# A state space layer without the product with the zero state, its entry weights loaded one stage earlier, and attention's stack copies all started by SyncE

## The chip, the cores and the metric

One Trainium2 chip, one core. The kernel is one launch for the whole model; the metric is the device time of that launch in microseconds (us), the median of the runs shown. Engines: TensorE (PE: matmuls; PEld: its weight loads), VectorE (DVE), ScalarE (ACT), GpSimd (POOL) and SyncE (SP, which only starts transfers here). The profile is one execution taken by the hardware profiler.

## The reference

Two rows of 1024 tokens with 512 channels go through four layers, each as `x = x + layernorm(layer(layernorm(x)))`: causal attention (32 heads of 16), a gated FFN whose weights are multiplied by low rank factors (FFN0), a state space layer, and a gated FFN (FFN1). The state space layer is what the change is mostly about:

```
proj = hidden @ in_proj_w.T            # gate | x,B,C | dt
hbc  = silu(conv4(x,B,C))              # causal, 4 taps per channel
dt   = softplus(dt + dt_bias); dA = exp(-dt * exp(A_log))
state = state * dA + (dt * x) B        # state0 = 0, for each token
y    = C . state + D * x
out  = (rmsnorm(y) * norm_weight * silu(gate)) @ out_proj_w.T
```

It has 64 heads of 64 in 8 groups, each group with one B and one C of 128.

## The kernel before, in words

Everything is fp32; a product is made of three fp32r matmuls from values split into hi and lo (hi x hi, lo x hi, hi x lo), so 12 matmuls of 512 columns make one product with K = 512. Each engine has its own program; semaphores order them. The outer loop runs over the 2 rows of the batch, and in each over the stages ATT, PROJ, FFN0, STEPS_DT, MAMBA, FFN1. `leave(engine, b, phase)` counts an engine out of a stage; `enter(engine, b, phase)` waits until all five engines have left the stage before. It is needed where a buffer of a new stage lies over one of an old stage.

**State space, MAMBA.** `m_group(g, first, last)` of each engine does one group of 8 heads in 8 chunks c of 128 tokens (TT = 8). A chunk on PE is, in this order (L986 to L1046): decays (L976, L977), B turned and the C-B product into bank 3 (L998, L999), the convolved projections of this or the next group (`PROJ_AT`: two in chunks 0 and 2 of each half, one in 1 and 3; `wide`, L928), with the last normed chunk turned in between (`turn_out`, L940), the product of C with the state (L1020, bank 6), the gate (`wide`, L928) with the 8 heads (L959, bank 7) between its matmuls, the out projection of the chunk before (`project_out`, L928, bank 3) with the next x turned in between (`turn_x`, L949), and the state update (L1046, bank 6). A bank of the two that projections and gate share is free when the use two before it has been read (`bank_read`): ahead of the gate of chunk 0 that is the convolution (DVE, L1684 to L1687) of the chunk's first projection.

What the other engines do for a chunk: ACT copies x_tm (L1283) and b_tm (L1286), takes the exponent of the decays (L1262), the first tap of a convolution (L1247), yt_hi (`turned_hi`, L1257), the silu's tanh (L1252), scales the state product into yv in 8 pieces (L1315), the gate's tanh (L1318), and the sum of squares (L1321); then splits weights (`split_hi`, L1236; wy is first scaled, L1234). In chunk 0 the first two splits of wy wait until the out projection is done. DVE: `masked` (L1703, L1706), convolutions, yt_lo (`turned_lo`, L1711), yv plus bank 7 (L1764), plus xd (L1767), gate (L1769), `gather` of the out projection from bank 3 into Y (L1717, L1719), state plus bank 6 (L1788), yn (L1791). In chunk 0 of a group DVE clears the state (L1739). POOL: xdt, xw, xd (L2061 to L2067), lo parts of weights (L2038), state times decay (L2078), decay terms (L2044), and the root of the mean square (L2090, L2092).

**The entry, STEPS_DT.** PE takes the product of the first half of the tokens with the dt weights (`steps_in(0)`), then six projections `project(0, 0, ft)`, with `steps_turn(0)` ahead of ft = 1, the turning of the second half's normed tokens, `steps_in(1)` behind ft = 2, `steps_turn(1)` behind ft = 3 and the decay sums (L902) behind ft = 4. SP loads wdt, dt_bias, a_log, d_skip (L552), cpar (L562) and m_raw (L560) after all engines have left FFN0. POOL then splits wdt (L1889, L1891).

**Attention.** Heads go by quads t = 0 to 7, two quads for each f = 0 to 3. Queries and keys of f are projected in four blocks (f, 0..3) of 12 matmuls (L595 to L597); weights come by `load_qk(f)` (L461, L463) and are split by POOL, the query half before (f, 0), the key half before (f, 2). `stack(t)` copies their hi and lo parts, SBUF to SBUF, into rows of stack_q and stack_k by 24 transfers (L309). The stacks of t = 2, 3 use the second buffers, which lie over the value weights, so they wait for `v_used`. SP starts all copies but those of t = 3, which ACT starts between its own steps. The maxima of a quad are built from 48 `piece` products (L803) each reduced by DVE (L1602, L1607), turned (L810) and brought into the stack by `put_maxima` (L479), on which the first score (L826) of the quad waits. `attention_order()` writes the order of all blocks out by hand; 48 pieces of quad 0 and 6 of quad 1 come before the first score. part_hi of f = 1 lies over probs, so ACT's first exponents (L1213) wait for the stacks of t = 2 and 3.

## Time and profile before

| | before |
|---|---|
| median of 3 runs | 4067.1 us (4065.34 to 4072.07) |
| profiled execution, time | 4082.54 us |
| its span | 4080.8 us |
| granted clock of TensorE, mean | 0.925 |
| PE busy | 3809.3 us, 93% |
| DVE busy | 2732.6 us, 67% |
| ACT busy | 1686.5 us, 41% |
| POOL busy | 1805.8 us, 44% |
| chain that ended last | PE 81%, issue 7%, DVE 4% |

A share of busy time is an average over stages with different limits. A row of a timeline gives start, duration, engine, line, operation, what it writes <- what it reads, and in brackets the idle time of the engine before it with what ended it. Durations of matmuls include their pipeline, so neighbours overlap: their distance is the start of the next less the start of this one. Two lines name one thing where a helper is shared: L595 to L597 are all products of attention and FFN, L928 all wide products of the state space layer.

### The profile page before, as it was taken

The page shows a single profiled execution, that of the slowest core. Times are in us where ns is not written, and L with a number is a line of the kernel's source. Part 1 is how long each engine was busy: PE and PEld are TensorE (multiplying, and loading weights), DVE is VectorE, ACT ScalarE, POOL GpSimd, SP SyncE. Part 2 cuts the span into 40 slices and gives each one's busy share as a digit, 9 for nine tenths or more (in the row PEclk, how much of TensorE's full clock was granted, in tenths as well). Part 3 has the DMA queues.
Part 4 walks back from the last instruction along what each step waited for, and adds up shares of the span by engine and source line. Part 5 has one row for each costly group of instructions (what it writes and reads, how often), then busy time and mean ns, then how long its engine had stood idle before and what let it go on. Part 6 is the DMA issues. An engine that isn't in the chain of part 4 may idle for free.

```text
span 4080.8 us, 61636 instructions
## 1 busy us (share of the span) xinstructions
PE 3809.3 (93%) x18088; PEld 2768.1 (68%) x18088; DVE 2732.6 (67%) x5102; ACT 1686.5 (41%) x3555; POOL 1805.8 (44%) x1993
## 2 busy tenths in 40 slices
PE   7899899799999999979979998996999999999797
PEld 5444588577777777767754446874777777777586
DVE  4576455678777787764546754556778777787545
ACT  1344411355555555541214443114555555555412
POOL 2111444266555665643221124433666655665432
PEclk9767799899999999989987768998999999999899
DMA  4120111011010111001051301101111100110111
GB/s 104 31 49 27 34 48 40 24 37 35 29 27 25 31 36 28 23 26 57 24 116 27 61 15 33 48 32 34 27 37 31 31 21 25 36 34 18 52 39 36
DMA packets 84630, 151.95 MB, mean 37 GB/s; under 512 B 16488, under 2 KB 18616, under 8 KB 84432
## 3 DMA queue, kind: packets, MB, share of 16 engines
q1 hardware_dynamic: 80784, 142.23, 13.1%
q10 hardware_dynamic: 3648, 7.34, 0.7%
q8 instruction: 92, 1.51, 0.1%
q14 instruction: 106, 0.87, 0.1%
HBM read 119.37 MB, written 4.19 MB: 30 GB/s over the span
## 4 chain that ended last, share of the span: by engine, by line
PE 81%; issue 7%; DVE 4%; POOL 2%; DVEq 2%; ACT 1%; POOLq 1%; DMA 1%; SPq 1%; ACTq 0%; PEldq 0%; PEld 0%
PE banks L928 30%; PE banks L595 8%; PE banks L596 7%; PE banks L597 7%; PE banks L845 5%; PE banks L959 4%; PE banks L826 4%; PE banks L803 3%; PE banks L1020 2%; PE banks L1046 2%; PE banks L976 1%; PE banks L977 1%; PE banks L949 1%; PE banks L940 1%; DVEq L1690 1%
## 5 line engine op out<-in xcount | busy, mean ns | idle before, releaser
L1687 DVE SCALAR_TENSOR_TENSOR conv<-banks,cpar,conv 128x509 f32<-128x509 f32 (+2 forms) x576 | 428.1, 743 | 123.0 <-ACT conv L1247 106.0
L959 PEld LDWEIGHTS banks<-xdt,decay 128*128 128x128 f32 x2048 | 393.9, 193 | 65.8 <-DVE decay L1706 11.2
L1213 ACT ACTIVATE probs<-banks 128x1024 f32<-128x1024 f32 (+3 forms) x384 | 296.7, 809 | 328.9 <-PE banks L826 328.3
L1474 DVE TENSOR_TENSOR Y<-banks,Y 128x512 f32<-128x512 f32 x368 | 253.1, 691 | 164.3 <-PE banks L597 163.0
L595 PE MATMUL banks<-xhi,f_hi 128*128 128x512 f32 x800 | 325.8, 407 | 30.9 <-POOL f_lo L1891 16.6
L959 PE MATMUL banks<-xdt,decay 128*128 128x64 f32 x2048 | 342.0, 249 | 12.7 <-DVE decay L1706 9.3
L2012 POOL TENSOR_SCALAR_AFFINE_SELECT probs<-probs 128x256 f32<-128x256 f32 x256 | 103.8, 406 | 536.6 <-ACT probs L1213 536.2
L803 PE MATMUL banks<-stack_k,stack_q 48*128 48x512 f32 (+3 forms) x768 | 320.5, 500 | 13.8 <-DVE mx L1607 6.8
L1602 DVE CUSTOM_DVE_ANT_0 banks<-banks,mask_qk 128x128 f32<-128x128 f32 (+3 forms) x512 | 249.3, 500 | 117.7 <-PE banks L803 113.2
L596 PE MATMUL banks<-xhi,f_lo 128*128 128x512 f32 x800 | 320.8, 401 | 0.0
L597 PE MATMUL banks<-xlo,f_hi 128*128 128x512 f32 x800 | 320.6, 401 | 0.0
L928 PE MATMUL banks<-xhi,wx_hi 128*128 128x512 f32 x720 | 310.4, 431 | 0.0
L826 PE MATMUL banks<-stack_q,stack_k 50*128 50x512 f32 (+3 forms) x768 | 292.0, 487 | 5.7 <-DVE mx L1602 3.0
L928 PE MATMUL banks<-xhi,wx_lo 128*128 128x512 f32 x720 | 295.9, 411 | 0.0
L928 PE MATMUL banks<-xlo,wx_hi 128*128 128x512 f32 x720 | 295.5, 410 | 0.0
L826 PEld LDWEIGHTS banks<-stack_q,stack_k 50*128 50x128 f32 x768 | 169.0, 249 | 168.3 <-issue 125.8
L928 PE MATMUL banks<-wg_hi,xhi 128*128 128x512 f32 x512 | 262.0, 512 | 21.8 <-DVE conv L1687 21.8
L2090 POOL TENSOR_SCALAR rg<-ss 128x1 f32<-128x1 f32 x128 | 25.1, 196 | 541.3 <-ACT banks L1321 541.3
L1889 POOL TENSOR_SCALAR f_hi<-f_raw 128x512 fp32r<-128x512 f32 x150 | 96.5, 643 | 324.2 <-PE banks L597 301.9
L928 PE MATMUL banks<-wg_lo,xhi 128*128 128x512 f32 x512 | 238.3, 465 | 0.0
L1132 ACT CAST h_hi<-hf 128x512 fp32r<-128x512 f32 x100 | 62.2, 622 | 408.2 <-DVE hf L1459 408.2
L928 PE MATMUL banks<-wy_hi,yt_hi 128*128 128x512 f32 x512 | 229.4, 448 | 0.7 <-POOL wy_lo L2038 0.7
(229 smaller groups left out, 10402.1 us busy)
## 6 DMA issues: line engine op xcount, KB each, us to landing
m_raw<-in_w_mamba SPq DMA_DIRECT2D x224, 256.0 KB, 2.6
f_raw<-in_w_ffn SPq DMA_DIRECT2D x50, 768.0 KB, 4.6
x_next<-in_x SPq DMA_DIRECT2D x6, 1024.0 KB, 8.8
wqk_raw<-in_w_attn SPq DMA_DIRECT2D x8, 512.0 KB, 3.7
stack_q<-part_hi SPq DMA_DIRECT2D x64, 64.0 KB, 2.4
stack_k<-part_hi SPq DMA_DIRECT2D x64, 64.0 KB, 2.5
X<-in_x SPq DMA_DIRECT2D x4, 1024.0 KB, 6.5
out_y<-X ACTq DMA_DIRECT2D x4, 1024.0 KB, 5.1
```

Source lines behind the costliest of these rows:

```text
L595: pe.matmul(dst, a_hi(kt), w_hi(kt), start=first, stop=False)
L596: pe.matmul(dst, a_lo(kt), w_hi(kt), start=False, stop=False)
L597: return pe.matmul(dst, a_hi(kt), w_lo(kt), start=False, stop=last)
L803: pe.matmul(bank[RING_BANK[use]][:, 0:cols], stack_q[buf][base:base + ROWS, h, i * P:(i + 1) * P], stack_k[buf][base:base + ROWS, h, s * H ...
L826: r = pe.matmul(bank[h][:, at:at + w], stack_k[buf][base:base + ROWS + 2, h, j * P:(j + 1) * P], stack_q[buf][base:base + ROWS + 2, h, s * ...
L845: r = pe.matmul(bank[6][32 * h:32 * h + VW, lo:HALF], V[:, j, QUAD * t + h, :], probs[n % 2][:, h, at:at + w], start=j == 0, stop=j == CPH ...
L928: r = pe.matmul(dst, a(kt), w(kt), start=n == 0, stop=n == 3 * KT - 1)
L959: r = pe.matmul(bank[7][:, h * MP:(h + 1) * MP], decay[:, h, :], xdt[:, h * MP:(h + 1) * MP], start=True, stop=True, skip_group_check=True)
L1213: act.activation(probs[n % 2][:, 2 * p:2 * p + 2, 0:w], banks[:, 2 * p:2 * p + 2, 0:w], ACT.Exp, scale=1.0 / HD ** 0.5).then_inc(exp_done[ ...
L1474: dve.tensor_tensor(Y[:, i, :], bank[6 + i % 2], Y[:, i, :], ALU.add).then_inc(f["dn_used"], 1)
L1602: dve.tensor_tensor_reduce(out=src, in0=src, in1=mask_qk[:, HALF - cols:HALF], scale=1.0, scalar=NEG, op0=ALU.add, op1=ALU.max, accum_out= ...
L1687: r = dve.scalar_tensor_tensor(out=rest, in0=src[:, 0:HALF - lag], scalar=cpar[:, o:o + 1], in1=rest, op0=ALU.mult, op1=ALU.add)
```

## The change

- The state of a group starts at zero, so chunk 0 leaves out the clearing, the product of C with the state, its scaling on ACT, one of DVE's two adds and the decay of the state on POOL; the state after chunk 0 is a copy of bank 6. The semaphores' counts follow (7 a group where there were 8).
- In chunk 0 of every group but a row's first, PE does the out projection of the chunk before ahead of the gate. ACT's `turned_hi` and DVE's `turned_lo` therefore come ahead of the first convolution.
- wdt, its three rows, cpar and the first two m_raw are loaded by SP at the end of FFN0 and wdt is split by POOL in FFN0; the buffers have places outside FFN0's. In STEPS_DT, PE turns the second half's tokens after ft = 1 and turns its steps after ft = 2, and ACT and DVE follow.
- In attention a block has 4 pieces (12 blocks), "values" 5 to 7 alternate with (1, 2), (1, 3), and the 6 pieces of quad 1 stand between (2, 3) and (3, 0). POOL splits query and key weights of an f in one operation each, after the last block of the f before. SP starts the copies of t = 3, and `load_qk(3)` goes ahead of `stack(2)`.

The diff, cut to what the text speaks of, with the common indentation taken off (the rest names the buffers' new places and the same counts):

```diff
-    for at, (first, second) in enumerate(blocks_left):
+    blocks_left = [("values", 3), (1, 0), ("values", 4), (1, 1), ("values", 5), (1, 2), ("values", 6), (1, 3),
+                   ("values", 7), (2, 0), (2, 1), (2, 2), (2, 3), None, (3, 0), (3, 1), (3, 2), (3, 3)]
+    for block_ in blocks_left:
+        if block_ is None:
+            yield "maxima", 0
+            yield from some(2)
+            yield "maxima_out", 0
+            yield from some(AHEAD - 2)
+            continue
+        first, second = block_
         values = first == "values"
...
-        if (first, second) == (2, 3):
-            yield "maxima", 0
-        if (first, second) == (3, 0):
-            yield "maxima_out", 0
-        if 9 <= at < 14:
-            yield "copies", 5 * (at - 9), min(5 * (at - 8), 24)
-        count = 3 if at < 9 else 7 if at < 12 else 2 if (first, second) in ((3, 0), (3, 3)) else 0
-        if (first, second) == (3, 3):
-            yield from some(AHEAD - 2)
-        else:
-            yield from some(min(count, 2))
+        count = min(PER_BLOCK, len(pieces) - (NQ - 1) * NP) if len(pieces) > (NQ - 1) * NP else 0
+        yield from some(min(count, 2))
         yield ("values_out", second) if values else ("proj_lo", first, second)
-        yield from some(count - 2 if count > 2 else 0)
+        yield from some(count - min(count, 2))
...
-            for n in range(QUAD * 6):
-                copy_part(sp, t, n)
+            for h in range(QUAD):
+                src = slice(HD * (QUAD * par + h), HD * (QUAD * par + h + 1))
+                for dst, which, parts in ((stack_q[f % 2], 0, (part_hi, part_hi, part_lo)),
+                                          (stack_k[f % 2], 1, (part_hi, part_lo, part_hi))):
+                    for r, part in enumerate(parts):
+                        at = 64 * par + HD * r
+                        sp.dma_start(dst[at:at + HD, h, :].bitcast(F32),
+                                     part[f][src, which, :].bitcast(F32)).then_inc(stacked[f % 2][par][h], 16)
...
+        load_qk(3)
         held(sp, v_used, b + 1)
         ones_in(1)
         stack(2)
-        load_qk(3)
+        stack(3)
         put_maxima(0)
...
         for at in STACK_AT:
             sp.dma_start(lrc_raw[at:at + RANK, :], lr0_const).then_inc(F[0]["lr_const"], 16)
         ffn_loads(0, w_ffn0, NF0, True)
-        leave(sp, b, FFN0)
-        enter(sp, b, STEPS_DT)
-
+        enter(sp, b, FFN0)
         for dst, src in ((wdt_raw[:], w_dt), (dtb[:], dt_bias), (alog[:], a_log), (dsk[:], d_skip)):
             sp.dma_start(dst, src).then_inc(dt_w_in, 16)
-        leave(sp, b, STEPS_DT)
-
+        sp.dma_start(cpar[:], conv_par[0]).then_inc(cpar_in, 16)
...
-        sp.dma_start(cpar[:], conv_par[0]).then_inc(cpar_in, 16)
-        for n in range(CT):
-            m_load(0, n, n, n < 2)
+        for n in range(2):
+            m_load(0, n, n, True)
+        leave(sp, b, FFN0)
+        enter(sp, b, STEPS_DT)
+        for n in range(2, CT):
+            m_load(0, n, n)
+        leave(sp, b, STEPS_DT)
...
-                    pe.wait_ge(wqk_ready, b * 8 + 2 * f + which + 1)
+                if use_f == 0 and part == 0:
+                    pe.wait_ge(wqk_ready, b * 8 + 2 * f + 2)
...
-                pe.wait_ge(state_ready, it + 1)
-                if c == 0:
-                    pe.wait_ge(inter_used, START + it)
-                pe.matmul(bank[6][:], xbc[s][:, XT + 1, ck], state[:], start=True, stop=True
-                          ).then_inc(inter_done, 1)
+                if c:
+                    pe.wait_ge(state_ready, sm + c)
+                    pe.matmul(bank[6][:], xbc[s][:, XT + 1, ck], state[:], start=True, stop=True
+                              ).then_inc(inter_done, 1)
+
+                def out_ahead():
+                    if c == 1:
+                        pe.wait_ge(m_split, b * (MG * W_PER_G) + g * W_PER_G + W_PER_G)
+                    pe.wait_ge(bc_ready, START + it + 1)
+                    ahead = (c + 1) % CPH != 0
+                    project_out(it - 1, {2 + 2 * k: lambda k=k: turn_x(it + 1, c + 1, k) for k in range(XT)}
+                                if ahead else {})
+
+                if c == 0 and not start:
+                    out_ahead()
...
                 at += 1
 
-                if not start:
-                    if c == 1:
-                        pe.wait_ge(m_split, b * (MG * W_PER_G) + g * W_PER_G + W_PER_G)
-                    pe.wait_ge(bc_ready, START + it + 1)
-                    ahead = (c + 1) % CPH != 0
-                    project_out(it - 1, {2 + 2 * k: lambda k=k: turn_x(it + 1, c + 1, k) for k in range(XT)}
-                                if ahead else {})
+                if c:
+                    out_ahead()
 
                 if c < TT - 1:
-                    pe.wait_ge(inter_used, START + it + 1)
+                    pe.wait_ge(inter_used, START + sm + c)
...
-            if ft == 2:
+            if ft == 1:
                 norm_turn(b * 4 + 2, 2, half(1))
                 normed(b * 4 + 2, 1)
                 steps_in(1)
-            if ft == 3:
+            if ft == 2:
                 steps_turn(1)
             if ft == 4:
                 decay_sums()
...
         for what, *arg in ORDER:
-            if what == "copies":
-                first, last = arg
-                if first == 0:
-                    held(act, v_used, b + 1)
-                    held(act, part_lo_ready, b * 16 + 8)
-                    act.drain()
-                for n in range(first, last):
-                    copy_part(act, 3, n)
-            elif what == "proj_hi":
...
                 turned_yet = start
+                if c == 0 and not start:
+                    turned_hi(it - 1)
                 while uses[at][0] == "proj":
...
@@ -1294,7 +1294,8 @@
                     s1 = 1 if n < CT else 0
                     before_conv(bank[at % 2], p0 + n, n, s1)
                     if not turned_yet:
-                        turned_hi(it - 1)
+                        if c:
+                            turned_hi(it - 1)
                         turned_yet = True
...
                 act.wait_ge(yn_ready, START + it)
-                act.wait_ge(inter_done, START + it + 1)
-                act.wait_ge(gt_ready, (b * MG + g) * 2 + c // CPH + 1)
-                for h in range(HPG):
-                    own = slice(h * MP, (h + 1) * MP)
-                    r = act.activation(yv[:, own], bank[6][:, own], ACT.Identity, scale=gt[:, EC, c, h:h + 1])
-                r.then_inc(inter_used, 1)
+                if c:
+                    act.wait_ge(inter_done, START + (b * MG + g) * (TT - 1) + c)
+                    act.wait_ge(gt_ready, (b * MG + g) * 2 + c // CPH + 1)
+                    for h in range(HPG):
+                        own = slice(h * MP, (h + 1) * MP)
+                        r = act.activation(yv[:, own], bank[6][:, own], ACT.Identity, scale=gt[:, EC, c, h:h + 1])
+                    r.then_inc(inter_used, 1)
...
+        act.wait_ge(dt_w_in, (b + 1) * 64)
+        act.activation(neg_a[:], alog[:], ACT.Exp)
         held(act, cpar_in, (b * MG + 1) * 16)
         for n in range(2):
             split_hi(wx_hi[:, n, :], n, 0)
-        act.wait_ge(dt_w_in, (b + 1) * 64)
-        act.activation(neg_a[:], alog[:], ACT.Exp)
         normed_y(b * 4 + 1, half(1))
         for n in range(2, 4):
             split_hi(wx_hi[:, n, :], n, 0)
         first_conv(0)
+        normed_x(b * 4 + 2, 2, half(1))
         first_conv(1)
         first_tanh(0)
-        normed_x(b * 4 + 2, 2, half(1))
...
-            held(dve, inter_done, START + (b * MG + g) * TT)
-            dve.memset(state[:], 0.0).then_inc(state_ready, 1)
...
                 turned = start
+                if c == 0 and not start:
+                    turned_lo(it - 1)
+                    turned = True
...
-                dve.wait_ge(inter_used, START + it + 1)
-                dve.wait_ge(intra_done, START + it + 1)
-                dve.tensor_tensor(yv[:], yv[:], bank[7], ALU.add)
-                dve.drain()
-                dve.wait_ge(pool_x, START + it + 1)
-                dve.tensor_tensor(yv[:], yv[:], xd[:], ALU.add).then_inc(y_ready, 1)
+                if c == 0:
+                    dve.wait_ge(intra_done, START + it + 1)
+                    dve.wait_ge(pool_x, START + it + 1)
+                    dve.tensor_tensor(yv[:], xd[:], bank[7], ALU.add).then_inc(y_ready, 1)
+                else:
+                    dve.wait_ge(inter_used, START + sm + c)
+                    dve.wait_ge(intra_done, START + it + 1)
+                    dve.tensor_tensor(yv[:], yv[:], bank[7], ALU.add)
+                    dve.drain()
+                    dve.wait_ge(pool_x, START + it + 1)
+                    dve.tensor_tensor(yv[:], yv[:], xd[:], ALU.add).then_inc(y_ready, 1)
...
+                if c == 0:
+                    dve.wait_ge(st_mm, START + sm + 1)
+                    dve.tensor_copy(state[:], bank[6]).then_inc(state_ready, 1)
+                elif c < TT - 1:
                     dve.wait_ge(st_mm, START + sm + (c + 1))
-                    dve.wait_ge(state_dec, sm + (c + 1))
+                    dve.wait_ge(state_dec, (b * MG + g) * (TT - 2) + c)
                     dve.tensor_tensor(state[:], state[:], bank[6], ALU.add).then_inc(state_ready, 1)
...
+        steps_copy(0)
         add_y(b * 4 + 1, half(1))
         moments_x(b * 4 + 1, 1)
-        steps_copy(0)
         first_conv(0)
+        norm_lo(b * 4 + 2, half(1))
         first_conv(1)
         first_silu(0)
-        norm_lo(b * 4 + 2, half(1))
         steps_copy(1)
...
+        if i == 0:
+            held(pool, dt_w_in, (b + 1) * 64)
+            split(wdt_hi[:], wdt_lo[:], wdt_raw[:]).then_inc(dt_w_ready, 1)
...
         for what, *arg in ORDER:
-            if what == "proj" and arg[1:] in ([0, 0], [2, 0]):
-                f, which = arg[0], arg[1] // 2
+            if what == "proj" and arg[1:] == [0, 0]:
+                f = arg[0]
                 held(pool, wqk_in, (b * (NQ // 2) + f + 1) * 32)
                 if f > 0:
-                    held(pool, ring_done, b * RING + RING_ENDS.index(("proj", f - 1, 2 * which + 1)) + 1)
-                split(wqk_hi[:, which, :], wqk_lo[:, which, :], wqk_raw[:, which, :]).then_inc(wqk_ready, 1)
+                    held(pool, ring_done, b * RING + RING_ENDS.index(("proj", f - 1, 3)) + 1)
+                split(wqk_hi[:], wqk_lo[:], wqk_raw[:]).then_inc(wqk_ready, 2)
...
-                    pool.wait_ge(state_ready, it + 1)
-                    pool.wait_ge(inter_done, START + it + 1)
-                    pool.tensor_tensor(by_head(state[:]), by_head(state[:]), per_head(gt[:, ED, c, :]),
-                                       ALU.mult).then_inc(state_dec, 1)
+                    if c:
+                        pool.wait_ge(state_ready, sm + c)
+                        pool.wait_ge(inter_done, START + sm + c)
+                        pool.tensor_tensor(by_head(state[:]), by_head(state[:]), per_head(gt[:, ED, c, :]),
```

## Rows read from the trace of the kernel before

**Rows 1.** The page: busy time by engine; PE's granted clock by slice, in tenths.

```profile
PE 3809.3 (93%) x18088; PEld 2768.1 (68%) x18088; DVE 2732.6 (67%) x5102; ACT 1686.5 (41%) x3555; POOL 1805.8 (44%) x1993
...
PEclk9767799899999999989987768998999999999899
```

**Rows 2.** Waits of PE: waiting line <- releaser: total us, count, mean us.

```profile
PE banks L928 <- DVE conv L1687: 21.8, 14, 1.6
```

**Rows 3.** Windows, one group: us; PE, PEld, DVE, ACT, POOL; PEclk, DMA, GB/s.

```profile
945.00:1070.00 125.00, 123.42 (x616) 96.06 (x615) 98.43 (x152) 66.95 (x169) 75.92 (x77) 1.00 0.11 30
```

**Rows 4.** Timeline of PE, chunks 0 and 1 of one group.

```profile
952.70 1.02 PE L1020 MATMUL banks<-state,xbc 128*128 128x512 f32 x2
...
955.30 0.49 PE L928 MATMUL banks<-wg_hi,xhi 128*128 128x512 f32 x1 [1.58 <-DVE conv L1687]
...
959.90 0.48 PE L928 MATMUL banks<-wy_hi,yt_hi 128*128 128x512 f32 x1
...
963.21 1.02 PE L1046 MATMUL banks<-xw,b_tm 128*128 128x512 f32 x2
...
965.00 0.27 PE L998 MATMUL banks<-ident,xbc 128*128 128x128 f32 x1
...
967.44 0.27 PE L940 MATMUL banks<-ident,yn 128*128 128x128 f32 x1
...
974.01 0.47 PE L928 MATMUL banks<-wy_hi,yt_hi 128*128 128x512 f32 x1
```

**Rows 5.** Timeline of DVE, the same chunks.

```profile
955.03 0.68 DVE L1711 TENSOR_TENSOR yt_lo<-banks,yt_hi 128x512 fp32r<-128x512 f32 x1
...
960.20 0.69 DVE L1764 TENSOR_TENSOR yv<-yv,banks 128x512 f32<-128x512 f32 x1 [0.45 <-PE banks L959]
...
963.41 0.69 DVE L1719 TENSOR_TENSOR Y<-banks,Y 128x512 f32<-128x512 f32 x1 [1.16 <-PE banks L928]
...
973.19 0.68 DVE L1711 TENSOR_TENSOR yt_lo<-banks,yt_hi 128x512 fp32r<-128x512 f32 x1
```

**Rows 6.** Timeline of ACT, the same chunks.

```profile
963.51 0.72 ACT L1234 ACTIVATE m_raw<-m_raw,cpar 128x512 f32<-128x512 f32 x1 [1.10 <-PE banks L928]
...
966.13 0.58 ACT L1283 COPY x_tm<-banks 128x512 f32<-128x512 f32 x1
```

**Rows 7.** Timeline of PE, entry to the state space layer.

```profile
761.74 0.66 PE L595 MATMUL banks<-xhi,wdt_hi 128*64 128x512 f32 x1 [4.82 <-POOLq L277]
...
766.89 0.63 PE L595 MATMUL banks<-xhi,wx_hi 128*128 128x512 f32 x1
...
786.22 0.44 PE L595 MATMUL banks<-xhi,wdt_hi 128*64 128x512 f32 x1 [1.40 <-DVE xlo L1434]
```

**Rows 8.** Timeline of DVE, the same entry.

```profile
766.31 2.81 DVE L1441 TENSOR_TENSOR X<-X,Y 128x512 f32<-128x512 f32 x4 [4.05 <-ACT Y L1098]
...
792.38 0.69 DVE L1814 TENSOR_TENSOR dt_in<-banks,dtb 128x512 f32<-128x512 f32 x1 [2.50 <-PE banks L896]
```

**Rows 9.** Timeline of ACT, the same entry.

```profile
779.57 1.51 ACT L1112 ACTIVATE xn<-X,shift,rstd 128x512 f32<-128x512 f32 x2
```

**Rows 10.** Timeline of SP's queue, attention.

```profile
61.40 1.15 SPq L309 DMA_DIRECT2D stack_q<-part_hi  x2
...
76.77 0.59 SPq L309 DMA_DIRECT2D stack_k<-part_hi  x1
...
82.77 2.43 SPq L485 DMA_DIRECT2D stack_k<-ones  x4
...
102.57 0.38 SPq L461 DMA_DIRECT2D wqk_raw<-in_w_attn  x1
```

**Rows 11.** Timeline of PE, attention.

```profile
110.40 0.79 PE L595 MATMUL banks<-xhi,wqk_hi 128*128 128x512 f32 x1 [7.33 <-POOL wqk_lo L1891]
...
127.57 0.49 PE L826 MATMUL banks<-stack_q,stack_k 50*128 50x512 f32 x1 [1.52 <-DVE mx L1602]
```

**Rows 12.** Tile wqk_raw: durations in ns (min/median/max), first to last start in us.

```profile
L1891 POOL TENSOR_TENSOR wqk_lo<-wqk_raw,wqk_hi x16: 1260/1281/1298, 20.9 to 2138.3; 128x512 fp32r<-128x512 f32 x16
```

More of the change, by code:

```diff
@@ L158, in build @@
         with ExitStack() as s:
+            wdt_raw = sb("wdt_raw", [P, KT, MH], stack=s)
+            wdt_hi = sb("wdt_hi", [P, KT, MH], F32R, stack=s)
+            wdt_lo = sb("wdt_lo", [P, KT, MH], F32R, stack=s)
+            dtb = sb("dtb", [P, MH], stack=s)
+            alog = sb("alog", [P, MH], stack=s)
+            neg_a = sb("neg_a", [P, MH], stack=s)
+            dsk = sb("dsk", [P, MH], stack=s)
+        with ExitStack() as s:
             EC, WE, ED, DTH, AHI, ALO = range(6)
@@ L162, in build @@
             with ExitStack() as s2:
+                cpar = sb("cpar", [P, CT * (MK + 1) + XT], stack=s2)
                 m_raw = sb("m_raw", [P, 2, D], stack=s2)
@@ L169, in build @@
                 wy_lo = sb("wy_lo", [P, XT, D], F32R, stack=s2)
-                cpar = sb("cpar", [P, CT * (MK + 1) + XT], stack=s2)
                 gt = sb("gt", [P, 6, TT, HPG], stack=s2)
@@ L2030, in _ @@
                 enter(pool, b, STEPS_DT)
-                held(pool, dt_w_in, (b + 1) * 64)
-                split(wdt_hi[:], wdt_lo[:], wdt_raw[:]).then_inc(dt_w_ready, 1)
                 leave(pool, b, STEPS_DT)
```

24 lines of the change are left out of this document (5 added, 19 removed).

## The prediction

> **What bounds the kernel now.** I began with the page: TensorE (PE) is busy 93% of the span and its chain is 81% PE, so time can go only where PE waits, where it does needless work, or where its clock is low. The clock row says where the last is: from slice 2 to slice 5 (102 to 510 us, the attention of the first batch) 7, 6, 7, 7 tenths, and 9 in nearly all the state space layer [rows 1]. Then the waits of PE; the one that comes back evenly is 14 times 1.56 us, 21.8 in all, on VectorE's (DVE) convolution at L928 [rows 2]. One group takes 125 us, of which PE is busy 123.4 at full clock, so that wait is all its idle [rows 3]: there the layer is bound by PE. The timelines of the three places that the diff touches follow; the second batch repeats the first in all of them.
>
> State space, chunk 0 of a group [rows 4 to 6]: the product with the zero state starts at 952.70, then PE idles 1.58 until conv has emptied the gate's bank; gate 955.30 to 959.90 (4.60 us), out projection to 963.21 (3.31 us). Entry to the state space layer: PE waits 4.82 us for weights which SyncE (SP) loads only after FFN0, then runs at half clock (12 matmuls from 761.74 to 766.89, 0.43 us apart; at full clock they are 0.23 apart, as 963.21 minus 959.90 over 12, less four small turns, shows too) [rows 7]. Attention: PE waits 7.33 us at 110.40 because the last query and key weights were loaded at 102.57, behind 24 stack copies; the first score is at 127.57 [rows 10, 11].
>
> **Part 1, group heads (14 of the 16 groups).** From 952.70 to the state update at 963.21 PE now takes 10.51 us. Afterwards: out projection 3.31 from 952.70 to 956.0, gate 4.60 to 960.6. What must be ready: yt_lo, which now precedes the convolution (turned_hi 0.58 on ScalarE (ACT), 0.68 on DVE, so about 951.4); the gate's bank, whose convolution moves 0.6 later for the same reason, its end from 955.0 (where yt_lo starts, [rows 5]) to 955.65, still under the projection. So 2.6 us go: 1.58 wait and some 0.95 product (from the 10.51, less wait, gate and projection, 1.0). The memset, eight ACT scalings, one DVE add and POOL's decay multiply go too; each lay beside PE and I give them nothing by themselves.
>
> What is late next, in chunk 1. (a) PE needs bank 3 at 965.00, 1.8 after the state update begins, so at 962.4 after; DVE empties it 4.2 after the gate's end now (963.41 + 0.69), but 1.2 of that was waiting for the projection and 0.7 the second add, so 962.8 or 962.9 after: a new wait of 0.45. (b) ACT splits wy from 963.51 and then copies x_tm at 966.13; its start goes only to 962.3 (gate's end, tanh and add, square 0.8), 1.2 earlier where PE is 2.6 earlier. x_tm is done at 965.5; PE wants it at 965.35 or, with (a), later: 0.2. (c) The same ACT chain starts the decay exponent, DVE's masked product and convolution, and yt_lo, which ended at 973.87 just before PE's projection at 974.01. It ends at 972.3 after, PE is there at 972.1: 0.3. Together 0.95 of 2.6 comes back; 1.65 x 14 = **23.1 us**. Ends: 1.0 (all of the idle returns, only the product goes) and 2.6 (nothing returns); I take the value that the chain gives, near the middle.
>
> **Part 2, the two first groups.** There PE waits in the gate for DVE's masked product, which is not moved: the dropped product hides behind that wait, worth 0. One DVE add less (0.69 [rows 5]) lies in the chain to x_tm, on which PE then waits: 0.7 x 2 = **1.4**, ends 0 and 1.9.
>
> **Part 3, entry.** Loads of wdt, the three rows, cpar and the first two m_raw go into FFN0, behind the last FFN load on SP; nothing of FFN0 is queued behind them. POOL's split of wdt follows the last FFN split, where POOL has nothing due until the next variance: 0, at most its 1.2 us. DVE's step copy now precedes the add, so the turn no longer waits for the add and its statistics. PE's first step product starts at about 758.4 instead of 761.74. What ends next is the layer norm of the second half. DVE's add begins at 766.31 [rows 8]; the root that it hangs on comes 1.9 earlier, since on POOL the split of wx ahead of it is over sooner and the variance, ready at 762, ends the wait. So the statistics end at 770.4, the root at 771.8, and the turned tiles, which took 6.65 from the first xn at 779.57 [rows 9] to 786.22, take about 6.2 without a convolution and silu between them: second step product at 778.0 instead of 786.22. It comes after a wait of 5 us, so I take half clock for it (5.1, as in rows 7), then projection 2 (2.8), the turn (0.5): dt_in at 786.0 instead of 792.38 [rows 8]. Everything after it (softplus, decay sums, convolutions 3 to 5) hangs on dt_in, so 6.4 x 2 = **12.8**. Ends: 4.8 (only the wait for weights) and 8.5 (full clock).
>
> **Part 4, attention.** load_qk(3) goes ahead of stack(2), so the wait of 7.33 shrinks: both halves of f=2 are split after (1,3), under values 7; f=3 is split after (2,3), 3.7 us on POOL (two halves of 0.62 + 1.28 [rows 12]) beside maxima and six pieces (2.5): about 1.2 of wait, projections from 106 to 117.5. But the first score also needs put_maxima(0), and the first exponent needs stack(3), whose buffer source is probs. SP issues these in order. 24 copies take 61.40 to 77.36, 0.66 each [rows 10]. v_used falls at 82.77 now; with "values 7" one block later and four pieces a block it is 88.8. Ones 2.5, stack(2) and stack(3) 48 x 0.65 = 31.2, maxima 1.2, landing 2.1: first score at **125.8** instead of 127.57. So 1.8 x 2 = 3.6 gained; PE idles 8 us before it. The second batch starts up to 1.9 later as the query half no longer goes first (0 to 1.9; 0.8 taken). Full clock in the first 1.7 us of scores may be lost: 0.5 each. Sum **1.8**, ends a loss of 8 (copies 0.75 each, SP's queue as the bound) and a gain of 19 (rival 2).
>
> Here a rule speaks against a row. The Trainium skill, "DMA: Bandwidth & Descriptors", section "Issuing engines are not separate DMA queues", says that starting transfers on several engines saves only sequencer time, usually small beside the DMA. By it moving ACT's 24 copies to SP costs about nothing, which is rival 2; rows 10 give 0.66 of queue time each, and 24 in a row are not small. Another, "TensorE: Matmul & The Clock Gate", section "HAM oscillation", has PE come back slow after a wait; the scores run at a low clock already [rows 1], so by it the sum would lose no more than the 0.5 a batch taken above.
>
> **Sum.** 23.1 + 1.4 + 12.8 + 1.8 = 39.1 us. The profiled execution took 4082.5 with a span of 4080.8, so 4043.4; the median of the three runs shown is 4067.1, 15.4 below it, and its forecast is **4028**.
>
> **Rivals.** (1) Chunk 1 has more slack than I read: all 2.6 stays, 14 x 0.95 = 13.3 more, 4015. For it: DVE works beside a less busy POOL; against: rows 5 and 6 leave it under 0.2. (2) SP's queue does not end last; first score after the projections, at 118: 7.8 x 2 more, 4012. Against: rows 10. (3) The waits of chunk 1 eat all the idle: 14 x 0.95 for the product, so 9.8 less gain, 4038. For it: three chains (a to c) are each tight, and POOL's au_lo too. (4) Slower: attention loses clock. Its granted clock of 0.67 over slices 2 to 4 [rows 1] means a third of 306 us at 2.4 GHz, the rest at 1.2. The idle before the scores and a new order of pieces could move which stretches are granted. If a third of those 102 us per batch went to the low level, PE's work in them would take 34 us more, 68 in all, less 39: 4096. It decides from 20 us a batch. Against: both batches show nearly the same pattern though they start differently.
>
> **How the numbers follow.** Forecast 0.55, rival 1 0.14, rival 2 0.06, rival 3 0.19, rival 4 0.06 (slower by over 0.2% in 0.04 of it). A measurement tells about 0.2%, 8.1 us, from no change. Every case but rival 4 gains over 8.1 us; I keep 0.01 of them for the band, where their errors could add up. Faster 0.93, same 0.03, slower 0.04. The forecast's own spread is 12 us either way (part 1 from 1.2 to 2.4 a group, part 3, some us of attention's clock); with rivals 1 and 3 taken in and the outer part of 2 and 4 left out the range is 4008 to 4046.
>
> **What would show it.** No L1020 in chunk 0 and no idle ahead of the gate; instead short waits at L998 on the gather of Y, at L940 on x_tm and ahead of L928 on yt_lo in chunk 1; groups every 123.3 us (125.0 would refute part 1). The first wdt product close behind the last xlo, a_all some 6 us sooner. In attention two full trains of 24 copies on SP, and PE idle some 8 us before the first score, released by mt_lo; if it is released by DVE or starts at 118, part 4 is wrong. I am wrong altogether if attention's PEclk tenths fall, or if chunk 1 idles over 2 us.

## The result and the profile after

| | before | after |
|---|---|---|
| median | 4069.59 us (4 runs, 4065.34 to 4074.09) | **4004.05 us** (4 runs, 4000.12 to 4016.49) |
| ratio | | 0.9844, 95% interval 0.9819 to 0.9869 |
| profiled execution: span, mean granted clock | 4080.8, 0.925 | 4000.4, 0.939 |

65.5 us less; the forecast was 39.1 less, 4028, with a range of 4008 to 4046. The result lies 4 us below that range. Measured again beside the experiments, the changed kernel took 4018.8, 4014.0 and 4021.1 (medians on three chips): all 19 of its executions have a median of 4016.5 and a mean of 4014.0, and 68 of the kernel before 4070.1 and 4070.2. So the first four lie some 12 us below the rest of the evidence, and the gain to be explained is 56 us in the mean. The page of after, parts 1 and 2 (before: [rows 1]):

```profile
PE 3750.0 (94%) x18056; PEld 2736.6 (68%) x18056; DVE 2683.5 (67%) x5070; ACT 1664.6 (42%) x3427; POOL 1788.6 (45%) x1961
...
PEclk9867999899999999999997779998999999999899
```

PE is busy 59 us less, though only 32 matmuls fewer run. The clock row says most of why: slices 2 to 5 stood at 7, 6, 7, 7 and stand at 8, 6, 7, 9 here. The timelines of PE, cut at the same instructions in both profiled executions, give the time by stage (both batches), and windows of 4 us the time at 1.2 GHz within it:

| stage | before, us | after, us | at 1.2 GHz, before | after |
|---|---|---|---|---|
| attention's first product to its second score | 97.4, 98.8 | 95.9, 95.8 | 10, 15 | 6, 11 |
| to the last score | 311.3, 308.1 | 288.6, 302.6 | 198, 188 | 135, 172 |
| to the end of FFN0 | 313.7, 313.6 | 312.2, 312.0 | 24, 24 | 14, 14 |
| to the first step product | 9.2, 9.2 | 5.8, 5.8 | 4, 4 | 1, 1 |
| to the first state update | 74.7, 74.7 | 71.1, 71.1 | 30, 30 | 30, 30 |
| to the last state update | 961.9, 961.9 | 946.3, 948.0 | 3, 3 | 0, 3 |
| to the end of FFN1 | 241.8, 241.8 | 240.3, 242.0 | 27, 27 | 24, 27 |

28 of the 80 us between these two executions lie in the score stretch (the row "to the last score"), in which the diff moves nothing: there PE was 79 us less at 1.2 GHz.

**A group.** One group in the windows (before: [rows 3]), then PE's timeline from its last chunk (before: [rows 4]):

```profile
926.85:1049.85 123.00, 122.47 (x614) 95.62 (x614) 95.05 (x150) 65.72 (x160) 74.98 (x75) 1.00 0.11 31
```

```profile
1026.18 1.02 PE L1020 MATMUL banks<-state,xbc 128*128 128x512 f32 x2
...
1049.85 0.65 PE L1052 MATMUL banks<-xw,b_tm 128*128 128x512 f32 x1
...
1051.99 0.33 PE L999 MATMUL banks<-ident,xbc 128*128 128x128 f32 x1
...
1054.64 0.33 PE L940 MATMUL banks<-ident,yn 128*128 128x128 f32 x1
...
1061.57 0.50 PE L928 MATMUL banks<-wy_hi,yt_hi 128*128 128x512 f32 x1 [0.20 <-POOL wy_lo L2050]
```

Groups take 122.9 where they took 124.8. No L1020 stands in chunk 0 and nothing waits ahead of the gate. From the state update, B is turned 2.14 later (1.79 before), the normed chunk 4.79 (4.23), the projection 11.72 (10.80): the waits that the forecast named (a), (b) and (c) cost 0.35, 0.21 and 0.36, together 0.92, of which 0.95 was forecast. Only (c) ends with another engine than forecast: POOL's lo part of wy, and DVE's yt_lo had ended only 0.08 before it.

**The entry and the scores.** PE's step products, DVE's dt_in, then the two places of attention (before: [rows 7, 8, 11]):

```profile
732.72 0.69 PE L595 MATMUL banks<-xhi,wdt_hi 128*64 128x512 f32 x1 [1.40 <-DVE xlo L1436]
...
752.57 0.69 PE L595 MATMUL banks<-xhi,wdt_hi 128*64 128x512 f32 x1 [1.40 <-DVE xlo L1436]
```

```profile
760.05 0.69 DVE L1825 TENSOR_TENSOR dt_in<-banks,dtb 128x512 f32<-128x512 f32 x1 [2.46 <-PE banks L896]
```

```profile
106.04 0.28 PE L810 MATMUL banks<-ident,mx 128*32 128x128 f32 x1 [3.90 <-DVE mx L1614]
...
125.53 0.78 PE L826 MATMUL banks<-stack_q,stack_k 50*128 50x512 f32 x1 [5.18 <-DMA stack_q<-mt_lo]
```

```profile
122.61 0.52 SPq L477 DMA_DIRECT2D stack_q<-mt_hi  x1
123.17 0.59 SPq L477 DMA_DIRECT2D stack_q<-mt_lo  x1
```

FFN0 ends 25.60 earlier after (last product 726.94, not 752.54). On the clock of before the three entry rows stand at 758.32, 778.17 and 785.65, where 758.4, 778.0 and 786.0 were forecast. The first score was forecast at 125.8 and starts at 125.53, behind SP's 48 copies. PE idles 5.18 us ahead of it where some 8 were forecast, as 3.90 already went at the turn of the maxima.

In the trace of before, though, a score had already started at 124.82. The one at 127.57 that I took for the first [rows 11] is the second, with four of the six pieces of quad 1 and a wait between the two:

```profile
124.82 0.50 PE L826 MATMUL banks<-stack_q,stack_k 50*128 50x512 f32 x1
```

So the first score of the first batch came later with the change, not earlier. Second against second score, from the batch's first product, the gain is 1.5 and 3.0 us in the two batches.

### The profile page after: what moved, and what is told of

It reads as the page before. It is cut to its first block, busy times and chain, and to the rows that moved or that the text cites. A ratio compares the mean times of both kernels' runs of the same rounds, so it can differ in the third digit from the quotient of the medians.

```text
span 4000.4 us, 61382 instructions
## 1 busy us (share of the span) xinstructions
PE 3750.0 (94%) x18056; PEld 2736.6 (68%) x18056; DVE 2683.5 (67%) x5070; ACT 1664.6 (42%) x3427; POOL 1788.6 (45%) x1961
## 3 DMA queue, kind: packets, MB, share of 16 engines
q1 hardware_dynamic: 82320, 145.38, 13.6%
## 4 chain that ended last, share of the span: by engine, by line
PE 77%; issue 8%; POOL 5%; DVE 3%; SPq 2%; POOLq 1%; ACT 1%; DMA 1%; DVEq 1%; ACTq 0%
PE banks L928 29%; PE banks L595 8%; PE banks L596 7%; PE banks L597 7%; PE banks L845 4%; PE banks L959 4%; PE banks L826 4%; PE banks L803 3%; PE banks L1052 2%; PE banks L1020 2%; POOL wy_lo L2050 2%; SPq L470 1%; PE banks L949 1%; PE banks L976 1%; PE banks L977 1%
## 5 line engine op out<-in xcount | busy, mean ns | idle before, releaser
L826 PE MATMUL banks<-stack_q,stack_k 50*128 50x512 f32 (+3 forms) x768 | 279.5, 469 | 15.0 <-DMA stack_q<-mt_lo 12.7
```

Source lines behind the costliest of these rows:

```text
L826: r = pe.matmul(bank[h][:, at:at + w], stack_k[buf][base:base + ROWS + 2, h, j * P:(j + 1) * P], stack_q[buf][base:base + ROWS + 2, h, s * ...
```

## The experiments

All kernels' executions, 183 in all, lie on parallel lines of time against mean granted clock: 0.001 of clock is 2.5 us (least squares with one slope; scatter about the lines 2.4 us). "Equal clock" below is a kernel's distance to the kernel before, read between two such lines at one clock, so that what the mean clock did is taken out. Its uncertainty (one standard error) is 0.6 us for the changed kernel and 0.7 to 1.1 for the others.

| kernel | runs | mean us | mean clock | equal clock |
|---|---|---|---|---|
| before | 68 | 4070.2 | 0.9295 | 0 |
| changed (first runs, e4, e9, e15) | 19 | 4014.0 | 0.9329 | -47.4 |
| e1 attention alone | 12 | 4058.0 | 0.9320 | -5.8 |
| e2 heads alone | 6 | 4043.8 | 0.9298 | -25.5 |
| e3 entry alone | 8 | 4049.6 | 0.9311 | -16.5 |
| e12 heads and entry | 5 | 4025.3 | 0.9298 | -44.1 |
| e11 buffers moved | 10 | 4063.9 | 0.9304 | -4.0 |
| e7 product dropped | 6 | 4091.2 | 0.9233 | +5.5 |
| e8 projection ahead | 12 | 4067.9 | 0.9304 | +0.1 |
| e5, e16 copies by ACT | 9 | 4006.7 | 0.9340 | -52.1 |
| e6 maxima later | 6 | 4018.4 | 0.9312 | -47.5 |
| e10 query half first | 5 | 4009.5 | 0.9316 | -55.3 |
| e13 pieces late | 5 | 4020.8 | 0.9306 | -46.5 |
| e14 pieces early | 12 | 4055.6 | 0.9337 | -4.0 |

### One part at a time: e1, e2, e3, e4

The kernel before with the diff's attention parts alone (e1), its `m_group` parts alone (e2), its buffers and STEPS_DT parts alone (e3), and the whole again (e4).

> The kernel before with the attention part of the change alone. Theory A: the gain beyond the forecast is made by the attention part, whose new order gives the score stretch more of the full clock; then this kernel gains 15 to 22 us and PEclk of the scores is 0.72 to 0.77 where before it was 0.68 and 0.70. Theory B: the clock of the score stretch varies from execution to execution or with its start, whatever the order; then only the earlier scores count (1.3 us a batch), it gains 1 to 5 us, and the granted clocks of its runs lie among those of the kernel before.

Ratio 0.9978 (0.9960 to 0.9996), 4056.5 median: 12.2 us less in the mean, of which 5.8 at equal clock and the rest by a clock higher by 0.0025, so between A and B.

> The kernel before with the state space groups' part alone (no product with the zero state, out projection ahead of the gate). Both theories: groups every 122.9 us instead of 124.8, 14 x 1.92 = 27 us, and 1 to 4 for the two first groups, so 27 to 31 us. If it gains 35 or more, the clock of a stretch that it does not touch went with it (theory B). The forecast on record had 24.5.

0.9935 (0.9912 to 0.9959). Groups take 123.1, 25.5 us at equal clock. Both theories asked for 27 or more; the forecast's 24.5 was nearer.

> The kernel before with the entry part alone (weights and rows loaded in FFN0, steps turned earlier). Both theories: 3.4 us before the first step product and 3.6 behind it, per batch, so 13 to 15 us; the forecast on record had 12.8. Theory B allows 5 us more or less by the clock of attention.

0.9947 (0.9928 to 0.9966). 16.5 us at equal clock. By the stages 12.6 of them lie between the end of FFN0 and the first state update (3.4 and 3.4 in the first batch, 3.5 and 2.4 in the second); and the groups, not touched, took 124.63 instead of 124.81.

> The changed kernel once more, as the sum to which e1 to e3 are compared on one chip. Theory A: e1 + e2 + e3 add up to it within 5 us (near 65 us), and its scores have PEclk over 0.72 in both batches. Theory B: its total varies by 10 us with the clock, and the parts sum to 45 to 50 only.

0.9867 (0.9842 to 0.9892), 4018.8. At equal clock the parts sum to 47.8 and the whole is 47.4: they add up, and to less than the first result said. Windows over the scores of the first batch, of the first profile of the changed kernel and of e4, the same program:

```profile
125.50:414.70 289.20, 275.65 (x1529) 124.32 (x1529) 196.86 (x615) 147.58 (x190) 57.09 (x127) 0.77 0.18 36
```

```profile
125.50:432.40 306.90, 296.25 (x1530) 131.50 (x1528) 197.97 (x615) 147.73 (x190) 56.94 (x127) 0.69 0.17 34
```

The same work took 17.7 us longer at a granted clock of 0.69 instead of 0.77, while DVE, ACT and POOL were busy for the same time. So the clock of the scores does differ between executions of one program, as theory B says. Why it does, no run tells.

### The two halves of the group's head: e7, e8

e7 drops the product, with the projection behind the gate as before; e8 moves the projection and keeps the product. The first diff is against the changed kernel's `m_group`, the second, cut, against the kernel before:

```diff
 e7, PE (ACT and DVE in their old order)
-                        if c == 0 and not start:
-                            out_ahead()
...
-                        if c:
+                        if not start:
                             out_ahead()
```

```diff
 e8, PE
                         pe.matmul(bank[6][:], xbc[s][:, XT + 1, ck], state[:], start=True, stop=True
                                   ).then_inc(inter_done, 1)
+                        if c == 0 and not start:
+                            out_ahead()
                         bank_read(g, at, uses)
...
```

> The kernel before without the product with the zero state and what hangs on it, but the out projection behind the gate and ACT and DVE in their old order. Theory A (PE then only waits longer for the convolution): the wait ahead of the gate grows from 1.58 to about 2.5 us, groups stay at 124.8, and only the two first groups gain (1 to 4 us in all). Theory B (each part is worth its own share): groups take 123.9, 13 us more.

Neither. Ratio 1.0051 (1.0032 to 1.0070): **slower by 21 us**. The wait grows to 2.44 as theory A says, and then the gate takes 6.17 us instead of 4.59, so a group takes 126.4. PE's gate in e7, and the windows around the same gate one group earlier, which starts at 950.5:

```profile
1077.21 0.49 PE L928 MATMUL banks<-wg_hi,xhi 128*128 128x512 f32 x1 [2.44 <-DVE conv L1691]
```

```profile
948.00:950.00 2.00, 0.02 (x1) 0.00 (x0) 1.92 (x4) 0.78 (x1) 2.00 (x3) 1.00 0.14 40
950.00:952.00 2.00, 1.54 (x7) 1.25 (x7) 2.00 (x4) 0.63 (x1) 1.68 (x2) 0.90 0.66 218
952.00:955.00 3.00, 3.00 (x13) 2.71 (x12) 2.70 (x6) 0.00 (x0) 0.00 (x0) 0.50 0.01 3
955.00:958.00 3.00, 3.00 (x18) 2.53 (x18) 1.12 (x2) 1.00 (x2) 0.00 (x0) 0.99 0.00 0
```

Behind the 2.44 us of idle PE runs some 3 us at 1.2 GHz (24 us a batch in e7's seven groups); behind the 1.58 us of [rows 4] it did not, in any of the 14 groups. So in the kernel before, the useless product kept PE's idle time short, and PE kept its clock.

Between these two lengths the outcome is not fixed. In the last group, chunk 4, PE waits 2.02 to 2.10 us for DVE's state add in every kernel but e1's. Fourth run of the changed kernel, then e16, second batch:

```profile
3723.90 1.12 PE L1020 MATMUL banks<-state,xbc 128*128 128x512 f32 x2 [2.09 <-DVE state L1799]
```

```profile
3728.12 1.12 PE L1031 MATMUL banks<-state,xbc 128*128 128x512 f32 x2 [2.09 <-DVE state L1818]
```

Behind the first PE keeps 2.4 GHz and takes 13.6 us from state update to state update; behind the second it runs 3.4 us at 1.2 GHz and takes 15.2. Of the 34 such waits in the 17 profiles other than e1's, 11 brought the low clock and 23 did not, both also within one trace (after: 2.10 did, 2.09 did not). (The Trainium skill, "TensorE: Matmul & The Clock Gate", section "HAM oscillation", has idle gaps bring the slow clock, as these rows show; the waits of its example are 3 to 5 us, longer than these.)

> The kernel before with the out projection ahead of the gate in chunk 0, and the product with the zero state kept. Theory A: the 1.58 us wait goes and the product stays; the chunk-1 waits give back less than the 0.92 seen with both, about 0.5: groups of 123.7, 14 x 1.1 = 15 us. Theory B (the chunk-1 waits follow PE's earliness one for one): groups of 124.2, 8 us.

Neither again: 0.9998 (0.9982 to 1.0014), groups of 124.8. The head gains 1.9 us and chunk 1 gives 1.9 back. PE's waits in e8, total, count and mean:

```profile
PE banks L998 <- DVE Y L1728: 13.6, 14, 1.0
```

With the product kept, DVE has the second add and ACT the eight scalings ahead of the gather of Y, so the wait that is under 0.35 in the changed kernel is 1.0 here, and those behind it grow too. So dropping the product alone costs 21 us, the move alone gives 0, and both together give 25 (e2). Without its partner neither takes PE's idle time away: it stands ahead of the gate in e7 and in chunk 1 in e8.

### Buffers alone, and all but attention: e11, e12, e9

e11 has the diff's buffer places and nothing else; e12 is the changed kernel with the attention of before; e9 the changed kernel.

> The kernel before with the buffers' new places alone (wdt, its rows and cpar), no instruction changed. Theory A (the 0.18 us a group that e3 gained in a stretch it does not touch comes from the places of the buffers): groups of 124.63 instead of 124.81, 3 us in all. Theory B (it comes from the order of loads or the code): groups of 124.81, time as before.

Theory A. 0.9972 (0.9957 to 0.9987), and no instruction was changed. One group in the windows of e11, against [rows 3]:

```profile
956.00:1080.60 124.60, 123.00 (x614) 95.77 (x614) 98.22 (x152) 66.95 (x168) 75.70 (x76) 1.00 0.11 31
```

The 0.18 us are spread evenly over the chunks and belong to PE's own pace; over all groups they make 3 of the 4.0 us at equal clock. Which buffer's place it is was not tried, and why it counts stays open. Less these 4.0, e3's entry is worth 12.5; 12.8 was forecast.

> The changed kernel with the attention of before (entry and heads parts together). Theory A (parts add up at equal clock, attention's part is worth its earlier scores alone): 41 us below the kernel before at equal clock, 6 above the changed kernel; its mean clock is that of the kernel before, up by 0.001 for the entry. Theory B (attention's part raises the clock): the same at equal clock, but its mean clock is below e9's by 0.003 or more.

0.9884 (0.9865 to 0.9902), 44.1 at equal clock, 3.3 short of the changed kernel; clock 0.9298, as in the kernel before. The time at equal clock is within 3 us of A's, and the clock is as B says.

> The changed kernel a third time, as the anchor for e10 and e12 on one chip. Theory A (the granted clock of the scores differs from execution to execution by chance): times between 4000 and 4025 again, on the same line with the mean granted clock as all runs so far, 47 us below the kernel before at equal clock, and the median between the two seen so far (4004 and 4019). Theory B (the change gives the scores more clock): its mean clock stays over that of the kernel before by 0.004 or more.

0.9857 (0.9836 to 0.9877), 4014.0, clock 0.9333. Times and line are as theory A says, but the mean clock is 0.0050 above that of the 15 runs of before on this chip and 0.0035 above e12's, as theory B says of both, though on four and five runs.

### SP's queue ahead of the scores: e5, e6, e10, e16

```diff
 e5: ACT starts the copies of t = 3
-                stack(3)
...
+                if copying:
+                    yield "copies", *copying
```
```diff
 e6: e5 and
-                           ("values", 7), (2, 0), (2, 1), (2, 2), (2, 3), None, (3, 0), (3, 1), (3, 2), (3, 3)]
+                           ("values", 7), (2, 0), (2, 1), (2, 2), (2, 3), (3, 0), None, (3, 1), (3, 2), (3, 3)]
```

> The changed kernel, but ACT starts the 24 copies of t = 3 again (5 each in blocks (2,0) to (2,3), 4 in (3,0)), SP only those of t = 2. Theory A (SP's queue ends last before the first score): the copies of t = 2 end near 107 us, the maxima go out as soon as they are turned, and the first score starts when the four blocks of f = 3 are done, near 118 instead of 125.5, with no wait for mt_lo: 7 us a batch, 14 in all at equal clock, near 4000. Theory B (the wait for mt_lo ends with something else, the turn of the maxima or ACT's queue, which now carries 16 us of issues among its own steps): first score between 122 and 126, gain under 6 us in all.

4001.1 (ratio 0.9844, 0.9820 to 0.9867). PE in e5:

```profile
105.65 0.28 PE L821 MATMUL banks<-ident,mx 128*32 128x128 f32 x1 [3.90 <-DVE mx L1633]
...
121.44 0.50 PE L837 MATMUL banks<-stack_q,stack_k 50*128 50x512 f32 x1
```

```profile
107.76 0.52 SPq L489 DMA_DIRECT2D stack_q<-mt_hi  x1
```

The maxima go out 14.9 us earlier and PE waits for nothing at the first score: SP's queue was what ended last. It starts at 121.4 and not at 118, because PE is at 1.2 GHz from 106.3 to 113.1, right behind the 3.90 us of wait at 105.65. (The Trainium skill, "DMA: Bandwidth & Descriptors", section "Issuing engines are not separate DMA queues", calls the sequencer time of starts usually small; with 48 starts of 0.65 us ahead of a waiting score it was the bound, and with 24 of them on ACT the scores began 4 to 5 us earlier in each batch.)

> As e5, and the turn of the maxima with the six pieces of quad 1 stands behind block (3,0) instead of ahead of it. Theory A: the 3.9 us that PE waits for DVE's last maxima ahead of the turn also go, as block (3,0) covers them: first score near 114, 11 us a batch, 22 in all at equal clock against the changed kernel. Theory B: the maxima then arrive later than the last block and the wait for mt_lo comes back: no better than e5.

```profile
105.63 0.49 PE L606 MATMUL banks<-xhi,wqk_hi 128*128 128x512 f32 x1 [3.86 <-POOL wqk_lo L1921]
...
112.15 0.28 PE L821 MATMUL banks<-ident,mx 128*32 128x128 f32 x1 [1.91 <-DVE mx L1633]
...
125.14 0.49 PE L837 MATMUL banks<-stack_q,stack_k 50*128 50x512 f32 x1
```

Theory B's outcome by another wait: POOL's undivided split of the weights of f = 3 ends when it did, so PE waits 3.86 for that instead, and 1.91 for the maxima as well. First score at 125.1; median 4018.7 (ratio 0.9873, 0.9848 to 0.9897), 47.5 at equal clock.

> As e6 (copies of t = 3 by ACT, maxima turned behind block (3,0)), and POOL again splits the query half of the weights ahead of block (f,0) and the key half ahead of (f,2), as in the kernel before. Theory A (what PE waited for in e6 was only the undivided split): the 3.86 us wait at (3,0) goes, that for the maxima stays under 2 us, PE keeps its clock in the last blocks, and the first score starts near 116; 5 us a batch better than e5, near 43 below the changed kernel's stage sum of both, that is 10 us less than e5 at equal clock. Theory B (another wait takes its place, the maxima's landing or the key half): first score at 120 or later, no better than e5.

```profile
107.85 0.39 PE L821 MATMUL banks<-ident,mx 128*32 128x128 f32 x1 [2.78 <-DVE mx L1633]
...
120.52 0.50 PE L837 MATMUL banks<-stack_q,stack_k 50*128 50x512 f32 x1
```

The 3.86 is gone, 2.78 stands at the maxima, PE's clock still drops, and the first score comes at 120.5: theory B's figure, 3 us better than e5 and e16 at equal clock and not 10. Median 4008.9 (ratio 0.9840, 0.9823 to 0.9858).

> The kernel of e5 again, as the candidate that beats both: 6 us below the changed kernel at equal clock (4.1 and 5.4 us earlier scores in its two batches), whatever the clock. If the earlier scores are all of it, its mean clock is the changed kernel's.

4010.2 (ratio 0.9851, 0.9828 to 0.9875). With e5, nine runs have a mean of 4006.7, 7 below the changed kernel's 19 (standard deviations of 8 us in both, so some two times its uncertainty): the lowest mean of all kernels run here, e10's being 4009.5. At equal clock the two are 4.7 below the changed kernel, where the scores of both batches together begin 8 to 9 us earlier. Where the other half goes stays open.

### The clock of the scores: e13, e14, e15

```diff
 e13: the changed kernel, None yields no pieces, and
+                if at >= 14:
+                    count = {14: 2, 17: AHEAD - 2}.get(at, 0)
```
```diff
 e14: the kernel before, and
-                count = 3 if at < 9 else 7 if at < 12 else 2 if (first, second) in ((3, 0), (3, 3)) else 0
+                count = 3 if at < 9 else 7 if at < 12 else AHEAD if at == 12 else 0
...
```

> The kernel before, but the six pieces of quad 1 stand in block (2,3) behind the turn of the maxima. Theory P: its mean clock rises from 0.929 to about 0.932 and it gains 5 us or more. Theory Q: clock at 0.929; the first score moves by under 1 us either way, time within 3 us of before at equal clock.

Theory P. 0.9961 (0.9946 to 0.9976), 4056.2: six products moved ahead of four blocks take 14.6 us off the mean. 4.0 of it is at equal clock; the clock is 0.9337 (12 runs) where it was 0.9295 (68 runs; 0.9299 in the 17 on this chip). PE in e14, the wait for weights and the second score:

```profile
111.43 0.79 PE L592 MATMUL banks<-xhi,wqk_hi 128*128 128x512 f32 x1 [6.48 <-POOL wqk_lo L1888]
...
125.73 0.39 PE L823 MATMUL banks<-stack_q,stack_k 50*128 50x512 f32 x1
```

The weights still come late and ACT still starts the copies of t = 3, and yet the second score starts at 125.7, against 127.57 before and 126.1 in the changed kernel. From the first product of the batch it is 95.4 us in both batches, where it was 97.4 and 98.8. So the six pieces by themselves bring the scores forward as much as the whole of attention's part.

> The changed kernel, but the six pieces of quad 1 stand where they stood before (two in block (3,0), four in (3,3)) instead of ahead of (3,0). Theory P (their place decides how the scores start and which stretches get the full clock): the mean clock falls from 0.933 to about 0.930 and the score stretches get longer by some 5 us each. Theory Q (something else of attention's part, or the few microseconds of wait ahead of the scores): clock stays at 0.933, time at equal clock within 3 us of the changed kernel.

0.9875 (0.9851 to 0.9899), 46.5 at equal clock, clock 0.9306 against 0.9329: P's direction, but five runs with a spread of 0.003 don't settle it alone. The second scores come 96.5 and 96.1 us after the batch's first product, where it is 97.5 and 98.5 in e12: the other edits bring them forward too, by 1.0 and 2.4.

> The changed kernel a fourth time, beside e13 on one chip. If the clock gain of attention's part is real, the mean clock of all its runs stays near 0.933 (it was 0.9334 over 14 runs, where the kernel before had 0.9292 over 52); if it was chance, these runs lie near 0.930.

0.9878 (0.9856 to 0.9899), clock 0.9316: halfway between the two outcomes, and five runs alone settle nothing. All kernels with the six pieces ahead of (3, 0) together, the changed kernel, e1, e5, e16, e14: 52 runs, 0.9331 (standard error 0.0004). All others but e7: 125 runs, 0.9300 (0.0003). Why the pieces' place changes which stretches of the scores get the full clock stays open; no run tells it.

## Why the prediction was wrong

It was wrong in size, not in sign. Against the first four runs it was 24 us too high; against the mean of 19 it was 14.

**Part 1, heads (24.5 with part 2).** Held: 25.5 at equal clock (e2). The 1.65 a group was 1.7 in e2, and the three chunk-1 waits came to 0.92 of 0.95. What failed is the bookkeeping beneath: I priced wait (1.58) and product (0.95) as shares that add up. e7 and e8 show +21 and 0. I saw no rival in which only one of the two takes hold; the number was right because both did.

**Part 3, entry (12.8).** Held: 12.5 by e3 less e11, and the three instants within 0.4 us. Missing was 4.0 us that comes with the buffers' places, which I had taken for nothing.

**Part 4, attention (1.8).** Size off, 5.8 at equal clock (e1), and the mechanism right only in part. SP's queue did release the first score, at 125.5 on mt_lo. But most of the gain is another thing. "First score at 125.8 instead of 127.57" compares it with the second score of before; between the two stood four pieces of quad 1 and the 1.52 us of wait for DVE's maxima, which moving the six pieces takes away. I gave that move nothing, and alone it is worth 4.0 of the 5.8 (e14), with the wait for weights and ACT's copies left as they were; the other edits without it are worth 2.4, uncertain by 1.5 (e13 against e12). The instant of 125.8 was right, the gain read off it was not. "1.8 x 2" failed too: I had read only the first batch's waits, and the second score of the second batch came 3.0 earlier. The "0.5 each" for lost clock came true in the first batch (PE is at 1.2 GHz from 124.0 on), but ahead of the second score PE was 5 us less at 1.2 GHz in either batch, which I had not counted. "0.8 taken" for the later start of the second batch held: its first wait was 14.5 us before and 14.7, 15.9, 14.8 and 15.8 in the four profiled executions of the changed kernel. (Two halves of 0.62 + 1.28 are 3.8 and not 3.7, which moves nothing.)

**The clock.** This is the step that failed most, and the one that put the result below the range. "Full clock in the first 1.7 us of scores may be lost: 0.5 each" and rival 4 let attention's clock only fall or stay. It rose: by 0.0035 in the mean of 19 against 68 runs, 8.8 us by the line, and e14 puts it on the six pieces of quad 1, an edit that I listed and costed at nothing. Why their place does that stays open. And I took "both batches show nearly the same pattern" for a fixed pattern. e4 shows that one program's scores take 289 or 307 us. The sign was in front of me: the profiled execution lay 15.4 above the median of three runs 7 us apart. The range had no term for it; the kernel before spreads from 4054 to 4088 over its 68 executions.

**The sum.** Forecast -39.1. At equal clock -47.4: heads +1.0, entry and buffers +3.7, attention +4.0 more than forecast, less 0.4. Clock -8.8 more. That is 56.2, the difference of the means. The rest to 65.5 is the first four runs, whose mean clock of 0.9360 was 0.0031 above that of all 19 (7.8 us), by chance as far as the runs show; their time at equal clock is that of the others. Rival 1 (all 2.6 stays, 4015) gives nearly the mean measured and is wrong: the waits came back as forecast.

## What to carry to other kernels

Price two edits that meet at one wait together: here one alone cost 21 us, the other gave nothing, and both gave 25. Before an operation that looks useless is dropped, look at what idle it leaves in PE and what clock PE had behind idles of that length, in more than one trace. Before two instants are compared, make sure that they are the same instruction in both traces: the first score here was the second of before. And where a stretch runs at a mixed granted clock, one profile and a few runs don't fix its time; compare kernels at equal mean clock, and put the spread of the clock into the range.

## What the runs showed of the hardware that was not expected

- Ahead of the gate, idle of 1.44 to 1.58 us left PE at 2.4 GHz in all 14 groups of before, and idle of 2.30 to 2.44 us brought 3.4 us at 1.2 GHz in all 14 of e7. Idle of 2.02 to 2.10 us at one place did either: the low clock in 11 of 34 cases.
- Attention's scores got a mean clock of 0.69 or 0.77 in two executions of one program; over 183 executions time follows mean clock at 2.5 us per 0.001.
- Six products moved ahead of four blocks changed the mean clock of the whole run from 0.9295 to 0.9337.
- Moving buffers, without a change to any instruction, made PE's groups 0.15% shorter (124.81 to 124.63), some 3 us over all groups.
